# A fused audio tower (patches, attention, mixture of experts): one q/k projection per batch, its parts placed by SBUF transfers, and a new order of a cycle's work

## The chip, the cores and the metric

One core of a Trainium2 chip. The metric is the device time of one execution in microseconds; the kernel before takes 269.61 us (median of 3 runs, 268.11 to 270.89).

## What is computed

Sixteen batches of 512 frames with 128 features. Per batch: three strided patch embeddings (patches of 8, 16 and 32 frames, half overlapping) give N = 221 tokens of 128 features; pre-norm attention with 8 heads of 16 is added; then, for the first 1024 tokens of the flattened batch only (T = 1024, so batches 0 to 4), a dropless mixture of 8 experts with top 2 is added.

```python
h = concat([patches_i(x) @ W_i.T + b_i + pos_i + scale_emb[i] for i in range(3)], axis=1)   # (16, 221, 128)
q, k, v = split(layernorm(h) @ w_qkv.T)            # 8 heads of 16
attn = softmax(einsum('bhnd,bhmd->bhnm', q, k) / sqrt(16), axis=-1)
h = h + (attn @ v).reshape(...) @ w_agg.T + b_agg
xg = layernorm(h).reshape(-1, 128)[token_ids]       # T tokens, sorted by expert
y = where(bin_ids == e, gelu(xg @ w1[e]) @ w2[e], y)   # for each of 8 experts
h = h + scatter_add(w * y)
```

## The kernel before

Each engine has its own instruction stream, written by hand in program order; semaphores join them. After a prologue that loads x and the weights and computes the first three token units, all engines run the same loop over cycles c = -2 to 15. Cycle c holds the attention of batch c, split in two blocks of tokens (128 and 93, `TILE_N`), the embedding of later batches, and in c = 7 to 14 one round of experts, n = c - 7, of three tiles of 128 tokens (two in n = 7).

*Token matmuls.* `PLAN[c] = (p1, p2, pm, p3, p4)` says how many matmuls of the token units 3 to 8 (264 in all, `LEFT`) `tok_some` issues at five places of cycle c. Units 3, 5 and 8 have 508 columns, unit 4 252, unit 6 504, unit 7 248. A unit's last matmul lets VectorE copy it out (`hT_evac`), which a new unit waits for since all share `e_ps`; each unit goes through x_hi w_hi, x_hi w_lo, x_lo w_hi.

*Attention on TensorE.* `s1(c, blk)` forms the scores of one block to find the row maxima: four PSUM banks `s_ps`, all of them, so VectorE's `maxima(c, 0)` must end before `s1(c, 1)`, and `maxima(c, 1)` before `place_max(c)`, which turns the negated maxima into `m_ps[:, 2]`. VectorE's `take_max` adds them into the low part of q. `s2(c, blk)` forms the transposed scores with the maxima already subtracted, again in all four banks, so ScalarE's `exps(c, 0)` must end before `s2(c, 1)`, and `exps(c, 1)` before `s1(c+1, 0)`. `pv(c-1)`, `aggregate(c-1)` finish the batch before.

*High and low parts.* q and k are each split into a rounded part and the rest. Of 32 rows per head, `q_hi` holds q_hi twice, `k_a` k_hi and k_lo, `q_lo` q_lo and the maxima, `k_b` k_hi and a unit row. To get q and k twice, `project_q` and `project_k` multiply with doubled weights (two fp32 matmuls each; from batch 8 on q is projected once and doubled by `q_double`, two shuffles on VectorE). ScalarE makes `q_high`, `k_high`, VectorE `q_low`, `k_unit`, `k_low`.

*Layer norm of batch c+2.* `h_turn`, a copy, `ln_stats` (VectorE), `stage1` (GpSimd, rstd), `ln_z` (VectorE), `z_turn`, `zT_copy`. Up to batch 8 `ln_z(c+2)` stands in cycle c and `z_turn(c+1)` behind `s1(c, 0)`; later `ln_z(c+1)` and `z_turn(c+1)` stand in the middle of cycle c.

*Experts, round n.* `zs_turn(n)` transposes the gathered tokens, `zsT_evac(n)` copies them and derives `slot_w` and `idx_u`; `hidden(n, i)`, a gelu, `down`; ScalarE weighs y, GpSimd scatters it with indirect transfers and copies the experts' weights. SP loads the tokens: `load_zs(0)` in c = 6, `load_zs(1)` and `load_zs(2)` in c = 7, then `load_zs(n+2)`; from the second on each waits for `idx_ready` of the round before. SP's queue is in order: what stands behind a waiting instruction waits too.

Of the kernel before, what the change touches and what calls it, by code (L numbers as in the profile page):

```python
# [176 lines left out]
def build(nc, x0, x1, wt, pos, bias, wqkv, wagg, bagg, consts, ew, ei, w1, w2, z0, out):  # L177
    with ExitStack() as ctx:
# [28 lines left out]
        q_hi = sb("q_hi", [P, 2, 2, NE], F32R)  # L207
        q_lo = sb("q_lo", [P, 2, 2, NE], F32R)
        k_a = sb("k_a", [P, 2, 2, NE], F32R)
        k_b = sb("k_b", [P, 2, 2, NE], F32R)  # L210
# [1460 lines left out]
```

## Time and profile before

| | |
|---|---|
| time, median of 3 | 269.61 us |
| profiled execution, its own time | 267.78 us |
| its span, first to last instruction | 266.0 us |
| TensorE (PE) busy | 251.3 us, 94% |
| VectorE (DVE) busy | 217.1 us, 82% |
| ScalarE (ACT) busy | 149.4 us, 56% |
| GpSimd (POOL) busy | 127.9 us, 48% |
| mean granted TensorE clock | 0.996 |
| chain that ended last | PE 65%, DVE 24%, POOL 2%, ACT 2%, DMA 2% |

The span is that of the instructions; the execution's own time holds 1.8 us more around it. A busy share is an average over stages. Matmuls are pipelined, so their durations overlap: what one costs is read from start to start. TensorE's weight loads (PEld) run beside its matmuls. In the chain, time is given by the engine that each step was on, followed back from the last instruction.

### The profile page before, as it was taken

Reading aid. Unit: us, or ns where it says so; the run is one execution under the profiler, and the core shown is the slowest. Engines: PE = TensorE matmul, PEld = TensorE weight load, DVE = VectorE, ACT = ScalarE, POOL = GpSimd, SP = SyncE. Lnnn points to the kernel's source line nnn. Section 1 sums busy time; section 2 is a strip of 40 time slices with the busy share of each in tenths; the row PEclk is TensorE's granted clock in tenths of the full one; section 3 lists DMA queues with packets and bytes.
Section 4 is the critical chain, followed back from the end, with each engine's and each line's share of the span. In section 5 each row is a group of like instructions: output and inputs, shape, how many; then the busy total and the mean of one; then the engine's idle time right before and its main releaser. Section 6 shows DMA issues by size and latency. Waiting matters only on the chain.

```text
span 266.0 us, 7015 instructions
## 1 busy us (share of the span) xinstructions
PE 251.3 (94%) x2759; PEld 206.8 (78%) x2759; DVE 217.1 (82%) x474; ACT 149.4 (56%) x244; POOL 127.9 (48%) x178
## 2 busy tenths in 40 slices
PE   7999989999899999999999999999999999998991
PEld 7799867777576779887777988888888797876771
DVE  3994679879989989788886979798989898888742
ACT  4770332825261525343437978796969696878350
POOL 4000031103348474748575165667676766855422
PEclk9999999999999999999999999999999999999998
DMA  6999300089301010101111103031313122122122
GB/s 210 418 391 464 130 1 0 2 246 316 90 22 27 28 30 28 27 28 27 30 44 38 40 10 54 19 51 29 51 29 53 27 40 34 16 34 19 30 22 44
DMA packets 17151, 21.30 MB, mean 80 GB/s; under 512 B 2392, under 2 KB 12224, under 8 KB 17088
## 3 DMA queue, kind: packets, MB, share of 16 engines
q1 hardware_dynamic: 12400, 17.68, 20.0%
q0 software_dynamic: 4336, 2.60, 7.9%
q10 hardware_dynamic: 384, 0.57, 0.7%
q8 instruction: 22, 0.36, 0.6%
q14 instruction: 9, 0.07, 0.1%
HBM read 16.44 MB, written 5.95 MB: 84 GB/s over the span
## 4 chain that ended last, share of the span: by engine, by line
PE 65%; DVE 24%; POOL 2%; DMA 2%; ACT 2%; issue 2%; SPq 0%; DVEq 0%; POOLq 0%; ACTq 0%
PE e_ps L1194 12%; PE s_ps L1286 10%; PE s_ps L1194 8%; PE m_ps L1400 7%; PE m_ps L1467 5%; DVE nmax L959 4%; PE m_ps L1268 3%; DVE k_b L935 3%; PE m_ps L1258 2%; PE e_ps L1482 2%; PE e_ps L1467 2%; DMA x_raw<-x 2%; DVE x_lo L821 2%; DVE o_tok L985 1%; PE m_ps L1374 1%
## 5 line engine op out<-in xcount | busy, mean ns | idle before, releaser
L959 DVE TENSOR_REDUCE nmax<-s_ps 128x4 fp32r<-128x884 f32 (+1 forms) x60 | 61.7, 1069 | 8.5 <-PE s_ps L1286 8.3
L632 ACT ACTIVATE probs<-s_ps 128x888 f32<-128x888 f32 (+1 forms) x60 | 51.2, 904 | 20.2 <-PE s_ps L1286 20.2
L527 POOL DMA_INDIRECT out<-y_sb,idx_u x23 | 36.9, 1602 | 26.4 <-DMA out<-y_sb,idx_u 23.5
L465 POOL TENSOR_TENSOR var_eps<-mv,eps_t 128x2 f32<-128x2 f32 x16 | 8.5, 531 | 62.7 <-DVE mv L914 62.6
L498 POOL DMA_INDIRECT z_slots<-z,slot_u x20 | 23.4, 1172 | 15.3 <-PE s_ps L1286 11.0
L1400 PE MATMUL m_ps<-probs,v_aug 128*32 128x221 f32 (+1 forms) x480 | 25.8, 353 | 0.0
L1482 PE MATMUL e_ps<-w_now,hidT 128*128 128x128 f32 x184 | 23.2, 276 | 0.0
L1286 PE MATMUL s_ps<-k_a,q_hi 32*128 32x222 f32 (+1 forms) x252 | 19.1, 309 | 3.7 <-DVE q_lo L929 2.2
L1482 PEld LDWEIGHTS e_ps<-w_now,hidT 128*128 128x128 f32 x184 | 22.4, 192 | 0.1
L1286 PEld LDWEIGHTS s_ps<-k_a,q_hi 32*128 32x128 f32 (+1 forms) x252 | 11.9, 169 | 12.5 <-issue 5.7
L693 ACT ACT_TABLE_LOAD x16 | 20.5, 1283 | 0.3
L473 POOL TENSOR_TENSOR hb<-h_sb,bagg_sb 128x256 f32<-128x256 f32 x16 | 11.7, 734 | 18.4 <-DVE z_sb L919 18.4
L1400 PEld LDWEIGHTS m_ps<-probs,v_aug 128*32 128x32 f32 (+1 forms) x480 | 14.0, 109 | 7.1
L1194 PE MATMUL e_ps<-x_hi,w_hi 128*128 128x248 f32 (+3 forms) x88 | 19.5, 349 | 0.0
L614 ACT COPY zT<-m_ps 128x221 f32<-128x221 f32 x16 | 5.5, 345 | 24.3 <-PE m_ps L1245 24.3
L1194 PE MATMUL e_ps<-x_hi,w_lo 128*128 128x248 f32 (+3 forms) x88 | 19.1, 345 | 0.0
L538 POOL COPY w_now<-w_sb 128x512 f32 x23 | 17.5, 891 | 2.6 <-issue 1.3
L973 DVE SCALAR_TENSOR_TENSOR q_lo<-q_lo,c_sb,m_ps 128x442 fp32r<-128x442 f32 x15 | 10.1, 675 | 9.3 <-PE m_ps L1374 9.3
L1194 PE MATMUL e_ps<-x_lo,w_hi 128*128 128x248 f32 (+3 forms) x88 | 17.7, 339 | 0.0
L1467 PE MATMUL m_ps<-zsT,w_now 128*128 128x128 f32 x120 | 16.9, 284 | 0.3 <-DVE zsT L1061 0.3
L549 POOL COPY w_now<-w_sb 128x512 f32 x23 | 16.8, 1025 | 0.4
L1286 PE MATMUL s_ps<-k_b,q_lo 16*128 16x222 f32 (+1 forms) x252 | 16.4, 267 | 0.0
(181 smaller groups left out, 602.2 us busy)
## 6 DMA issues: line engine op xcount, KB each, us to landing
w_raw<-wt SPq DMA_DIRECT2D x6, 512.0 KB, 9.8
x_raw<-x SPq DMA_DIRECT2D x6, 512.0 KB, 10.9
w_sb<-w SPq DMA_DIRECT2D x1, 2048.0 KB, 9.7
z_slots<-z SPq DMA_DIRECT2D x1, 1518.0 KB, 15.0
zs<-z_slots SPq DMA_DIRECT2D x7, 198.0 KB, 2.5
x_raw<-x SPq DMA_DIRECT2D x4, 256.0 KB, 5.3
out<-h SPq DMA_DIRECT2D x11, 64.0 KB
c_sb<-consts SPq DMA_DIRECT2D x1, 600.0 KB, 13.1
```

The costliest lines, as they stand in the source:

```text
L498: g.indirect_dma_start(z_dram, bass.IndirectOffsetOnAxis(ap=slot_u[0:n, col:col + 1], axis=0), z2[0:n, b % 2, t, k, :], None).then_inc(sca ...
L527: g.indirect_dma_start(rows, bass.IndirectOffsetOnAxis(ap=idx_u[:, at:at + 1], axis=0), y_sb[:, n % 2, i, :], None, compute_op=ALU.add).th ...
L538: g.tensor_copy(w1_now[:, i, :], w1_sb[:, bass.ds(e, 1), :].rearrange("p a f -> p (a f)")).then_inc(w1_ready, 1)
L549: g.tensor_copy(w2_now[:, i].rearrange("p c d -> p (c d)"), w2_sb[:, bass.ds(e, 1), :, :].rearrange("p a c d -> p (a c d)")).then_inc(w2_r ...
L632: s.activation(probs[0:n, blk, 2 * f:2 * f + 2].rearrange("p t u n -> p t (u n)"), s_ps[0:n, 2 * f:2 * f + 2, 0:2 * NE], ACT.Exp, scale=DH ...
L693: s.activation(warm[func][:], c_sb[:, C_SGN:C_SGN + 1], func)
L959: v.tensor_reduce(nmax[0:n, blk, 2 * f:2 * f + 2, DH:DH + 2], src, AX_X, ALU.max, negate=True).then_inc(max_ready, 1)
L1194: mm = pe.matmul(dst, w_part[:, t, :], src, start=((u, k, i, c) == at_piece[0]), stop=((u, k, i, c) == at_piece[-1]))
L1286: mm = pe.matmul(dst[0:n, i, u * NE:(u + 1) * NE], a[rs, u, P * blk:P * blk + n], b[rs, u, :], start=start, stop=stop)
L1400: mm = pe.matmul(m_ps[32 * t:32 * t + 32, 0, r * N:(r + 1) * N], v_aug[0:n, b % 2, blk, HALF * r + t, :], probs[0:n, blk, t, r, 0:N], star ...
L1467: mm = pe.matmul((e_ps if i % 2 else m_ps[:, 1])[:, c * P:(c + 1) * P], w1_now[:, i, c * P:(c + 1) * P], zsT[:, i, :], start=True, stop=True)
L1482: mm = pe.matmul(e_ps[:, i * P:(i + 1) * P], hidT[:, i, c, :], w2_now[:, i, c, :], start=(c == 0), stop=(c == FC - 1))
```

## The change

q and k are projected once, side by side (`project_qk`, two fp32 matmuls into one bank), and split once into `qk` = (q_hi, k_hi, q_lo, k_lo): `qk_high` on ScalarE, `qk_low` on VectorE. Six transfers per batch, issued by SP (`place_qk`), put these parts into the rows of `pair_a` (even rows q_hi and k_hi, odd rows q_hi and k_lo) and `pair_b` (even rows k_hi and q_lo; the unit rows are set once by `set_units`). `k_high`, `k_unit`, `k_low`, `q_double` are gone. `take_max` now writes `q_max`, so `s1` and `s2` read different tensors. The low products use 32 rows instead of 16. Blocks are of 104 and 117 tokens. The experts' weights are loaded in four pieces in cycles 1 to 4. On TensorE `pv` stands directly between the two halves of `s1`, with the tokens behind; `hidden(n+1, 0)` and `z_turn(c+2)` end the cycle; `PLAN` is new. `ln_stats`, `ln_z`, `v_copy` and, for n >= 0, `keep_h` move, and aggregate's result lies in bank 0, so `pv(b)` waits for the residual of b - 1. A line of "..." stands for what is left out.

```diff
-N0, N1 = P, N - P
+N0 = 104
+N1 = N - N0
...
-PLAN = {-2: (3, 11, 0, 0, 0), -1: (2, 4, 0, 1, 3), 0: (18, 8, 0, 10, 12), 1: (2, 5, 2, 5, 10), 2: (2, 5, 2, 5, 10),
-        3: (2, 5, 2, 5, 10), 4: (4, 10, 4, 10, 20), 5: (4, 10, 4, 10, 20), 6: (2, 5, 2, 5, 10)}
+PLAN = {-2: (3, 11, 0, 0, 0), -1: (4, 6, 0, 16, 20), 0: (4, 8, 0, 6, 10), 1: (2, 6, 2, 5, 6), 2: (3, 7, 2, 4, 6),
+        3: (4, 9, 4, 8, 8), 4: (4, 10, 4, 8, 14), 5: (4, 8, 4, 8, 12), 6: (2, 5, 2, 5, 10)}
...
+            def place(b, pair, odd, u, parts):
+                half = HALF * DH
+                to, of = pair[odd:P:2, b % 2, u], qk[half * u:half * (u + 1), parts]
+                sp.dma_start(to.bitcast(F32), of.bitcast(F32)).then_inc(qk_placed[b % 2], 16)
+            def place_qk(b):
+                sp.wait_ge(qk_hi_ready, b + 1)
...
+                    sp.wait_ge(s2_done, 2 * b - 2)
+                for u in range(2):
+                    place(b, pair_a, 0, u, slice(0, 2))
+                sp.wait_ge(qk_lo_ready, b + 1)
+                for u in range(2):
+                    place(b, pair_a, 1, u, slice(0, 4, 3))
+                for u in range(2):
+                    place(b, pair_b, 0, u, slice(1, 3))
...
-            for c in range(BATCH + 1):
+            for c in range(-1, BATCH + 1):
                 n = c - E0
+                if c + 1 < BATCH:
+                    place_qk(c + 1)
+                if 1 <= c <= EXPERTS // 2:
+                    load_experts(2 * c - 2, 2 * c)
...
+            def qk_high(b):
+                act.wait_ge(qk_done, b + 1)
+                if b:
+                    act.wait_ge(qk_placed[(b - 1) % 2], 16 * PLACES * ((b - 1) // 2 + 1))
+                s.copy(qk[:, 0:2, 0:N], qk_ps()).then_inc(qk_hi_ready, 1)
...
+            def qk_low(b):
+                dve.wait_ge(qk_hi_ready, b + 1)
+                if b:
+                    dve.wait_ge(qk_placed[(b - 1) % 2], 16 * PLACES * ((b - 1) // 2 + 1))
+                v.tensor_tensor(qk[:, 2:4, 0:N], qk_ps(), qk[:, 0:2, 0:N].bitcast(F32),
+                                ALU.subtract).then_inc(qk_lo_ready, 1)
...
                 if c == BATCH - 1:
                     nmaxT_copy(c)
-                elif c >= 0:
-                    take_max(c)
+                elif c >= -1:
+                    qk_low(c + 1)
+                    if c >= 0:
+                        take_max(c)
...
                 if here:
                     s1(c, 0)
-                if ahead1 and c + 1 < LATE_Z:
-                    z_turn(c + 1)
-                if n > 0:
-                    hidden(n, 0)
                 if behind:
                     pv(c - 1)
-                tok_some(p1)
                 if here:
                     s1(c, 1)
-                if ahead1 and c + 1 >= LATE_Z:
-                    z_turn(c + 1)
+                tok_some(p1)
                 if n == 0:
                     zs_turn(0)
-                    project_q(c + 1)
+                else:
+                    hidden(n, 1)
+                if ahead1:
+                    project_qk(c + 1)
+                if n == 0:
                     hidden(n, 0)
-                hidden(n, 1)
+                    hidden(n, 1)
                 hidden(n, 2)
-                if ahead1 and n != 0:
-                    project_q(c + 1)
-                hidden(n, 3)
...
                 if here:
                     s2(c, 0)
-                if ahead1:
-                    project_k(c + 1)
                 tok_some(p3)
...
                 tok_some(p4)
+                if n >= 0:
+                    hidden(n + 1, 0)
+                if ahead2:
+                    z_turn(c + 2)
```

TensorE, cycle 4, from `pv(3)` to `aggregate(3)`, before. `L1194` are token matmuls, `L1258` and `L1268` the projections of q and k, `L1236` and `L1237` h_turn, `L1374` place_max; `s_ps<-k_a,q_hi` is s1, `s_ps<-q_hi,k_a` s2.

```order
L1400 MATMUL m_ps<-probs,v_aug 32x221 x16
L1194 MATMUL e_ps<-x_hi,w_hi 128x248 x4
L1286 MATMUL s_ps<-k_a,q_hi 93x222 x4
...
L1194 MATMUL e_ps<-x_hi,w_hi 128x248 x4
L1286 MATMUL s_ps<-q_hi,k_a 128x222 x8
L1286 MATMUL s_ps<-q_lo,k_b 128x222 x8
L1268 MATMUL m_ps<-zT,wqkv_sb 128x221 x2
L1194 MATMUL e_ps<-x_hi,w_hi 128x248 x10
L1286 MATMUL s_ps<-q_hi,k_a 93x222 x8
L1286 MATMUL s_ps<-q_lo,k_b 93x222 x8
L1430 MATMUL m_ps<-wagg_sb,o_T 128x128
```

The same place of the changed kernel; `L1381` is pv, `L1253` project_qk, `L1353` place_max, `L1410` aggregate.

```order
L1381 MATMUL m_ps<-probs,v_aug 32x221 x16
L1268 MATMUL s_ps<-pair_a 117x222 x4
...
L1194 MATMUL e_ps<-x_hi,w_hi 128x248 x4
L1253 MATMUL m_ps<-zT,wqkv_sb 128x221 x2
...
L1353 MATMUL m_ps<-ident_r,nmax 128x118
L1194 MATMUL e_ps<-x_hi,w_lo 128x248 x4
L1268 MATMUL s_ps<-pair_a 104x222 x8
L1268 MATMUL s_ps<-q_max,pair_b 104x222 x8
L1194 MATMUL e_ps<-x_hi,w_lo 128x248 x8
L1268 MATMUL s_ps<-pair_a 117x222 x8
L1268 MATMUL s_ps<-q_max,pair_b 117x222 x8
L1410 MATMUL m_ps<-wagg_sb,o_T 104x128
```

Nothing stands between pv and s1's second half now, and between s2's halves k's projection and two of ten token matmuls are gone.

SP's queue around cycle 7, before (`L410` and `L413` store h, `L420` is load_zs, the one in the middle load_zs(1) and load_zs(2)):

```order
L420 DMA zs<-z_slots 128x3x132 [waits scattered1,scattered0]
L410 DMA out<-h 128x128 [waits h1_ready]
L413 DMA out<-h 93x128
L420 DMA zs<-z_slots 128x3x132 [waits slot_w_ready,idx_ready,zs_turned] x2
L410 DMA out<-h 128x128 [waits h1_ready]
```

And of the changed kernel (`L414` is place):

```order
L450 DMA zs<-z_slots 128x3x132 [waits scattered1,scattered0]
L440 DMA out<-h 104x128 [waits h1_ready]
L443 DMA out<-h 117x128
L414 DMA pair_a<-qk 64x444 [waits s2_done,qk_hi_ready]
L414 DMA pair_a<-qk 64x444
L414 DMA pair_a<-qk 64x2x222 [waits qk_lo_ready]
L414 DMA pair_a<-qk 64x2x222
L414 DMA pair_b<-qk 64x444 x2
L450 DMA zs<-z_slots 128x3x132 [waits slot_w_ready,idx_ready,zs_turned] x2
L440 DMA out<-h 104x128 [waits h1_ready]
```

The six transfers of batch 8 now stand ahead of load_zs(1) and load_zs(2).

TensorE at the end of cycle 2 of the changed kernel, from aggregate(1) to the first scores of batch 3; `x_lo,w_hi` are the first token matmuls of unit 6 that read x_lo:

```order
L1410 MATMUL m_ps<-wagg_sb,o_T 104x128
L1411 MATMUL m_ps<-wagg_sb,o_T 117x128
L1259 MATMUL m_ps<-wqkv_sb,zT 104x128
L1260 MATMUL m_ps<-wqkv_sb,zT 117x128
L1194 MATMUL e_ps<-x_hi,w_lo 128x504 x3
L1194 MATMUL e_ps<-x_lo,w_hi 128x504 x3
L1242 MATMUL m_ps<-c_sb,z_sb 128x104
L1243 MATMUL m_ps<-c_sb,z_sb 128x117
L1268 MATMUL s_ps<-pair_a 104x222 x4
```

In the kernel before, the x_lo matmuls of unit 6 begin in cycle 3; here three of them stand ahead of batch 3's first scores, and z_turn(4) behind them.

## Rows read from the trace of the kernel before

**Rows 1.** Busy time by stretch of cycles: length, engines, clock, DMA share.

```profile
core 0: us, PE busy (x) PEld busy (x) DVE busy (x) ACT busy (x) POOL busy (x), PEclk, DMA share, GB/s
40.35:53.16 12.81, 12.12 (x131) 10.54 (x132) 12.12 (x28) 6.97 (x10) 1.86 (x4) 1.00 0.01 1
53.16:136.84 83.68, 82.77 (x902) 63.94 (x901) 72.49 (x157) 33.68 (x54) 44.31 (x64) 1.00 0.24 72
136.84:151.62 14.78, 14.23 (x171) 11.72 (x170) 12.25 (x29) 10.05 (x16) 4.90 (x8) 1.00 0.21 50
151.62:234.54 82.92, 80.32 (x1002) 68.68 (x1001) 72.91 (x160) 66.20 (x117) 57.39 (x71) 1.00 0.23 34
```

**Rows 2.** Timeline of cycle 4: start, duration, engine, operation.

```profile
95.52 0.38 PE L1286 MATMUL s_ps<-k_a,q_hi 32*128 32x222 f32 x4
...
96.29 2.06 DVE L959 TENSOR_REDUCE nmax<-s_ps 128x4 fp32r<-128x884 f32 x2
...
98.81 0.35 PE L1286 MATMUL s_ps<-k_a,q_hi 32*93 32x222 f32 x4
...
102.52 0.49 PE L1286 MATMUL s_ps<-q_hi,k_a 32*128 32x222 f32 x8
...
103.24 1.01 PE L1268 MATMUL m_ps<-zT,wqkv_sb 128*128 128x221 f32 x4
...
103.36 1.72 ACT L632 ACTIVATE probs<-s_ps 128x888 f32<-128x888 f32 x2 [2.11 <-PE s_ps L1286]
...
105.34 0.45 PE L1286 MATMUL s_ps<-q_hi,k_a 32*93 32x222 f32 x8
```

**Rows 3.** Chain that ended last, merged: start, duration, what.

```profile
58.25 1.13 PE e_ps L1194 x5
...
96.58 1.64 PE m_ps L1400 x32
...
99.47 0.94 PE m_ps L1258 x4
100.63 1.16 PE e_ps L1194 x10
```

**Rows 4.** Timeline, TensorE, cycle -1.

```profile
35.36 1.01 PE L1258 MATMUL m_ps<-zT,wqkv_sb 128*128 128x221 f32 x4
```

**Rows 5.** Timeline, cycle 2: the second half of s1, VectorE's tail.

```profile
71.03 0.35 PE L1286 MATMUL s_ps<-k_a,q_hi 32*93 32x222 f32 x4 [0.58 <-DVE nmax L959]
...
77.62 0.25 DVE L914 BATCH_NORM_AGGREGATE mv<-stats 128x2 f32<-128x6 f32 x2
...
79.41 0.60 DVE L919 TENSOR_SCALAR z_sb<-h_sb,mv,rstd 128x128 f32<-128x128 f32 x2 [0.30 <-POOL rstd L467]
...
80.26 1.65 DVE L821 TENSOR_TENSOR x_lo<-x_raw,x_hi 128x1024 fp32r<-128x1024 f32 x1
```

**Rows 6.** Timeline of cycle 7; then the answer on tile zs: issue, landing.

```profile
141.89 0.22 DVE L1063 TENSOR_SCALAR idx_u<-zs,c_sb 128x3 uint32<-128x3 f32 x1
...
142.18 0.38 SPq L420 DMA_DIRECT2D zs<-z_slots  x1
...
144.72 0.55 PE L1450 MATMUL e_ps<-c_sb,zs 128*128 128x128 f32 x3
...
L420 SPq DMA_DIRECT2D zs<-z_slots x8: 371/372/380, 137.0 to 215.1; - x8
...
DMA to landing us min/median/max: 2.1/2.5/3.7
```

**Rows 7.** Timeline, cycle 10 and the start of 11.

```profile
186.98 0.55 DVE L1061 COPY zsT<-e_ps 128x384 f32<-128x384 f32 x1
...
188.02 1.95 PE L1482 MATMUL e_ps<-w_now,hidT 128*128 128x128 f32 x16
...
192.93 0.19 PEld L1286 LDWEIGHTS s_ps<-k_a,q_hi 32*128 32x128 f32 x4 [0.59 <-DVE q_lo L929]
```

**Rows 8.** Timeline, VectorE, cycle 13.

```profile
223.55 0.61 DVE L919 TENSOR_SCALAR z_sb<-h_sb,mv,rstd 128x128 f32<-128x128 f32 x2 [0.98 <-POOL rstd L467]
```

More of the change, by code:

```diff
@@ L203, in build @@
         zT = sb("zT", [P, N])
[L207 to L210, printed above, removed]
+        qk = sb("qk", [P, 4, NE], F32R)
+        pair_a = sb("pair_a", [P, 2, 2, 2, NE], F32R)
+        pair_b = sb("pair_b", [P, 2, 2, 2, NE], F32R)
+        q_max = sb("q_max", [P, 2, NE], F32R)
         v_aug = sb("v_aug", [P, 2, 2, HEADS, 32])
@@ L297, in build, with q_hi, k_a, q_lo @@
             "p (b t u n) -> p b t u n", b=2, t=HALF, u=2)
-        def q_src(b):
-            return q_d[:] if b >= DOUBLED else m_ps[:, 0, 0:2 * N].rearrange("p (u n) -> p u n", u=2)
+        def q_hi(b):
+            return pair_a[:, b % 2, :, 0]
+        def k_a(b):
+            return pair_a[:, b % 2, :, 1]
+        def q_lo(b):
+            return pair_b[:, b % 2, :, 1]
+        def k_b(b):
+            return pair_b[:, b % 2, :, 0]
+        def qk_ps():
+            return m_ps[:, 0, 0:2 * N].rearrange("p (w n) -> p w n", w=2)
+        def agg_bank(b):
+            return e_ps[:, 2 * P:4 * P] if b == BATCH - 2 else m_ps[:, 0, 2 * P:4 * P]
         def pair_of(banks):
@@ L451, in _ @@
             g.memset(mhalf_t[:], -0.5)
-            for part in (q_hi, q_lo, k_a, k_b):
-                g.memset(part[:, :, :, N:NE].bitcast(F32), 0.0)
+            g.memset(qk[:, :, N:NE].bitcast(F32), 0.0)
+            g.memset(q_max[:, :, N:NE].bitcast(F32), 0.0)
+            g.memset(pair_b[:].bitcast(F32), 0.0)
             g.memset(nmax[:].bitcast(F32), 0.0)
@@ L594, in _ @@
                 scatter_y(n - 1, 2)
+                if n >= 0 and c + 2 < BATCH:
+                    keep_h(c + 2)
                 if 0 <= b < FFN_B - 1:
@@ L1302, in s1 @@
                 for u in range(2):
-                    four(s_ps, q_hi[:, b % 2], k_a[:, b % 2], blk, u, True, False)
-                    mm = four(s_ps, q_lo[:, b % 2], k_b[:, b % 2], blk, u, False, True, rows=DH)
+                    four(s_ps, q_hi(b), k_a(b), blk, u, True, False)
+                    mm = four(s_ps, q_lo(b), k_b(b), blk, u, False, True)
                 mm.then_inc(s1_done, 1)
@@ L1322, in s1_pair @@
                 for u in range(2):
-                    four(dst, q_hi[:, b % 2], k_a[:, b % 2], blk, u, True, False, heads)
-                    mm = four(dst, q_lo[:, b % 2], k_b[:, b % 2], blk, u, False, True, heads, DH)
+                    four(dst, q_hi(b), k_a(b), blk, u, True, False, heads)
+                    mm = four(dst, q_lo(b), k_b(b), blk, u, False, True, heads)
                 mm.then_inc(s1_done, 1)
```

250 lines of the change are left out of this document (89 added, 161 removed).

## The prediction

> **What bounds the kernel now.** I read the stretches first, then TensorE's timeline of one cycle of each kind, then the chain. A cycle runs from one s1(c,0), the first scores' first half, to the next. [rows 1] give the cycles: c0 12.81 us, c1 to c6 83.68, c7 14.78, c8 to c13 82.92; PE is busy for 82.77 of the 83.68 and 80.32 of the 82.92, at clock 1.00 throughout. So PE's instruction stream, in its written order, sets the pace; the others count only where PE has nothing to issue. One such place recurs late: s1(c,0) waits 0.59 for q_lo at the end of VectorE's k_b, k_a, q_lo tail [rows 7].
>
> **Prices.** On PE: pv 1.64; q or k projection 0.94 in the chain, 0.69 between starts (103.24 to the token matmuls after it), so I take 0.7; a token matmul 0.115 (248 or 252 columns) or 0.23 (504 or 508) [rows 3]. The two chained dependencies of a cycle are in [rows 2]: VectorE starts the maxima 0.77 after s1(4,0) starts and needs 2.06, so s1(c,1) cannot start before 0.77 + 2.06 + 0.06 = 2.89 after s1(c,0); and ScalarE's two exps start 0.84 after s2(4,0) and take 1.72, so s2(c,1), which reuses their banks, cannot start before 2.6 after s2(c,0). Before, PE covers both: z_turn, pv and tokens fill the first (s1(4,1) stands at 3.29), k's projection and 10 tokens the second (105.34 - 102.52 = 2.82).
>
> **What the change does to them.** It saves PE one projection of 0.7 per cycle up to c6 (four matmuls become two) and one matmul of about 0.37 later. VectorE loses k_b, k_a, the shuffles and gains one v copy; ScalarE loses k_a. That relief pays only where PE waited for it, the 0.59 of [rows 7]. Against it stand four costs.
>
> *1. Cycles -1 and 0: +4.0.* 46 instead of 10 token matmuls stand in c = -1. From the projection at 35.36 [rows 4]: 0.85 + 0.14 (h_turn) + 6 x 0.23 + 0.4 (v) + about 0.6 (hT_evac of unit 3, which now gates unit 4) + 36 x 0.115 + 0.33 (z_turn) puts s1(0,0) at 43.3 instead of 40.35 [rows 1]: +3.0. The six transfers hide here: q/k are split by about 37.6, the last issue is near 39, and landing within 4 is early enough. In c0 the 18 tokens between the halves are gone, so PE stands 2.25; lo_x behind the maxima delays the second maxima to 6.35. Adding the pieces: 0.64 + 2.25 + 0.59 + 0.5 + 0.99 + 1.0 + wait 0.4 + 0.26 + s2 with its wait 1.4 + 1.55 + 0.35 + 0.59 + 0.46 + 2.45 + 0.33 = 13.8 for 12.81: +1.0. Some of this is work moved, credited next.
>
> *2. c1 to c6: +2.6.* Off: six k projections, -4.2, and the moved tokens (29.2 of work for 32.8), -3.6. On: the first dependency is covered by s1 (0.64) and pv (1.64) alone, so PE waits 2.89 - 2.28 = 0.6 in each, +3.6. The second is covered by 4 to 8 tokens (0.9 to 1.3), leaving 0.6 to 0.85, +4.5. At c2 two VectorE effects come on top. The new order puts ln_stats, then the wait for GpSimd's rstd (77.87 to 79.41, 1.54, filled with k_b and k_a before, now empty), ln_z, v copy, lo_x (1.65) and the residual one behind the other [rows 5]; c1's tail then ends about 1.9 too late for the maxima of c2, and PE stands 0.6 + 1.9 ahead of s1(2,1), where it stood 0.58 before: beyond the 0.6 already counted, +1.3. And unit 6 started earlier, so its last three tokens of c2 are x_lo tokens: they wait for lo_x(9), which by the same addition ends 2.1 after PE gets there: +2.1. Sum -7.8 + 3.6 + 4.5 + 1.3 + 2.1 = +3.7. Adding starts along each cycle gives 2.2, since a block of tokens costs a gap at its borders, and some blocks are gone. I take 2.6, nearer the latter.
>
> *3. c7: +4.8.* The queue of SP is in order. load_zs(1) was issued at 142.18, 5.34 into the cycle, as soon as idx_u was there, and PE's zs_turn(1) ran at 144.72 just as it landed [rows 6]. Now it stands behind place_qk(8), whose third transfer waits for qk_low(8), which VectorE reaches behind the maxima of s1(7,1). These start behind zsT_evac(0) at about 5.2, end at 7.25, qk_low ends at 7.85; four issues at 0.37 put load_zs(1) at 9.35 and, landing in 2.5, at 11.85 (issue and landing: [rows 6]). PE is at zs_turn(1) at 8.4: it waits 3.4, and behind it on PE stand h_turn, s2(7,0), down and all the rest. After 11.85: 0.75 to s2(7,0) at 12.6, zsT 13.6, down 15.5, s2(7,1) 16.15, aggregate, v, down 18.5, then hidden(1,0) (0.96, moved in from c8) and z_turn 0.33: 19.6 for 14.78. load_zs(n+2) later is harmless: it is ready near 9.0, after the transfers are issued.
>
> *4. c8 to c13: +1.3.* Per cycle: -0.4 matmul, -0.5 of the wait for q_lo; +0.6 before s1(c,1); +0.15 for h_turn behind the third gelu; +0.4 before down, because zsT ends (186.98 + 0.55) and down used to start at 188.02 behind k's projection, which covered it [rows 7]. Together +0.3, +1.7 over six; c13's own 1.0 wait for rstd [rows 8] may go, hence 1.3.
>
> *5. c14: -1.0.* hidden(7,0) has moved to c13 and the waits ahead of s1(15,0) go. The tail is left as it is (0).
>
> Edits at nothing: N0 = 104 (a half costs PE 0.64 or 0.59, so the mean stays), 32 rows instead of 16 in the low products, the new order of zT, o_raw and the gelus on ScalarE (busy 66.20 of 82.92 in c8 to c13 [rows 1]), set_units in the prologue, where VectorE waits for the counts; if that cover fails it costs about 1. Weight loads in four pieces: they follow each cycle's transfers by half a cycle.
>
> **The transfers.** The trace has no SBUF-to-SBUF transfer. Nearest rows: zs, 198 KB, lands in 2.1 to 3.7 [rows 6], against 114 KB each here. From the last issue (about 8 into a cycle) to the next s1 there are 5 us: at 2.1 or 3.7 they cost nothing. Free below 5, each us above costs 15. The Trainium skill, "DMA: Bandwidth & Descriptors", Rules for kernel authors, warns that two transfers to disjoint partition halves serialize on the same engines; its fit in the section on the anatomy of one DMA (2.0 us plus bytes over 436 GB/s) makes, as an estimate of that page, 2.3 for one and about 3.6 for all six in series. By the page or by the zs row the sum is the same, but the rule is what would feed the second rival.
>
> **Sum.** 4.0 + 2.6 + 4.8 + 1.3 - 1.0 = +11.7: a span of 277.7 for 266.0. The profiled execution took 267.78, 1.83 below the median 269.61 of the runs shown; with the same difference the median becomes 281.3, said 281.
>
> **Rivals.** *PE work and VectorE relief decide (faster).* 22 fp32 projection matmuls at 0.37 are 8 us, five late waits of 0.6 another 3: 269.6 - 11 = 259. It needs PE not to stand ahead of s1(c,1) and s2(c,1); it decides if the two reductions take under 1.5 together instead of 2.06 and the exps under 1.0 instead of 1.72. The rows speak against it. A milder form, half the waits of parts 2 and 4 filled and no wait in c7: 281 - 4.8 - 7 = 269, no change. *The transfers land late (slower still).* At 7 us instead of under 4, 15 cycles wait 2: 281 + 30 = 311; at 5.5, 288. For it: six at once, 682 KB; against: 5 us of room. *GpSimd's rstd is late.* z_turn is now needed in the cycle of its ln_stats; as in c13 [rows 8], 1.0 for seven cycles: 288. Against: keep_h is now behind the last scatter, so stage1 can start by about 10. *load_zs(1) is not late*, everything else as forecast: 276.
>
> **Chances.** Forecast with its own range 276 to 286: 0.58. Without the c7 wait, 271 to 277: 0.12. Late rstd or transfers: 0.10. No change: 0.09. Faster: 0.11. A measurement of this kernel tells about 1% from no change. Faster by over 1% (under 267) 0.12, within 1% (to 272.3) 0.11, slower 0.77. Range 268 to 288.
>
> **What would show it.** s1(0,0) near 43; PE idle about 0.6 ahead of each s1(c,1), released by nmax, and 0.6 to 0.85 ahead of s2(c,1) in c1 to c6, released by probs; in c2 a wait of token matmuls for x_lo; in c7 one wait of over 3 us of zs_turn for the zs transfer, issued behind six transfers; cycles 8 to 13 near 14.1. Wrong if s1(c,0) waits for transfers, if z_turn waits for z_sb every cycle, or if the second halves start without a gap.

## The result, and the profile after

Four executions of the changed kernel took 283.24 us (282.32 to 285.85), four of the kernel before on the same chip 268.86 (268.01 to 270.89): ratio 1.054, 95% interval 1.044 to 1.064. It is slower, by 14.4 us where 11.7 were forecast. The profiled execution took 283.87 with a span of 281.8, against 266.0 before. Some executions of a kernel, whatever the kernel, run at a lower granted clock than its others, and the ratios leave them out: one of five of a3_fill and one of two of a4_late_places (the profiled one of each), two of ten of b2_plan_tok_zs, two of four of b3_and_hidden, two of six of c1_all_filled, and one of the eleven of the kernel before that ran beside it.

The first lines of the page after: span, busy time of the engines, and the clock of TensorE in 40 slices of 7 us.

```profile
span 281.8 us, 6982 instructions
...
PE 244.3 (87%) x2711; PEld 202.4 (72%) x2711; DVE 191.2 (68%) x420; ACT 140.2 (50%) x220; POOL 124.8 (44%) x177
...
PEclk9999999898899999999999689999999999999998
```

The stretches that answer to [rows 1]: cycle 0, cycles 1 to 6, cycle 7, cycles 8 to 13 (columns: bounds, length, busy time and instructions of PE, PEld, DVE, ACT, POOL, granted clock, DMA share, GB/s).

```profile
44.43:58.99 14.56, 11.82 (x107) 9.57 (x106) 10.58 (x24) 6.47 (x9) 1.71 (x3) 0.88 0.21 48
58.99:144.93 85.94, 73.84 (x862) 57.79 (x861) 63.19 (x144) 30.68 (x48) 39.14 (x63) 0.98 0.44 117
144.93:167.70 22.77, 17.02 (x178) 14.62 (x177) 11.36 (x26) 10.49 (x17) 7.95 (x14) 0.85 0.28 65
167.70:252.11 84.41, 76.87 (x990) 65.51 (x989) 61.07 (x133) 61.66 (x102) 57.34 (x69) 1.00 0.44 83
```

The change does take work off TensorE: 73.84 us in cycles 1 to 6 where [rows 1] had 82.77 (3.6 of the 8.9, by the prediction's price, are the 16 token matmuls dealt to earlier cycles). But 12.1 us of these cycles are now idle where 0.9 were. Who is waited for stands in the waits of the page after, TensorE's own, largest first (line of the instruction that waits, the one that releases it: us in total, times, longest):

```profile
PE s_ps L1268 <- DVE nmax L968: 10.0, 14, 2.2
PE e_ps L1430 <- DMA zs<-z_slots: 5.2, 1, 5.2
PE e_ps L1194 <- DVE hT L825: 4.4, 3, 1.8
PE s_ps L1268 <- ACT probs L663: 4.2, 7, 0.7
PE e_ps L1462 <- DVE zsT L1070: 2.7, 6, 0.5
PE m_ps L1236 <- ACT hidT L715: 1.6, 6, 0.4
PE e_ps L1194 <- DVE x_lo L840: 1.3, 1, 1.3
```

The same place as [rows 2] after, cycle 4 on TensorE, shows the two dependencies with their empty stretches, 0.63 for the maxima and 0.70 for the exps:

```profile
105.70 0.35 PE L1268 MATMUL s_ps<-pair_a 32*104 32x222 f32 x4
...
108.62 0.37 PE L1268 MATMUL s_ps<-pair_a 32*117 32x222 f32 x4 [0.63 <-DVE nmax L968]
...
112.70 0.46 PE L1268 MATMUL s_ps<-pair_a 32*104 32x222 f32 x8
...
113.36 1.18 PE L1194 MATMUL e_ps<-x_hi,w_lo 128*128 128x248 f32 x8
115.24 0.47 PE L1268 MATMUL s_ps<-pair_a 32*117 32x222 f32 x8 [0.70 <-ACT probs L663]
```

And cycle 7, which alone costs 8.0 us more than before: the chain of waits through it (start, length, what).

```profile
145.65 2.07 DVE nmax L968 x2
...
150.91 1.06 DVE nmax L968
151.97 0.54 DVE qk L953
152.52 0.62 SPq L414
153.13 0.04 issue
153.18 0.61 SPq L414
...
153.83 0.60 SPq L414
...
154.47 0.60 SPq L414
...
155.18 2.74 DMA zs<-z_slots
157.92 0.04 issue
157.96 0.90 PE e_ps L1430 x3
...
160.36 3.75 PE e_ps L1462 x16
```

Maxima, qk_low, four transfers of q and k, the transfer of zs, and only then zs_turn(1): as forecast. Not forecast is the last row: 16 matmuls of down take 3.75 us where [rows 7] have 1.95 for the same 16. The granted clock in the stretch behind the wait is 0.50 (1.2 GHz) for 6 us:

```profile
158.00:160.00 2.00, 2.00 (x21) 1.76 (x21) 0.67 (x2) 0.00 (x0) 0.00 (x0) 0.50 0.00 0
160.00:162.00 2.00, 1.93 (x16) 1.68 (x13) 1.90 (x10) 1.66 (x2) 0.75 (x2) 0.50 0.19 33
162.00:164.00 2.00, 2.00 (x10) 1.82 (x9) 1.22 (x4) 0.06 (x1) 1.45 (x3) 0.50 0.28 77
164.00:166.00 2.00, 2.00 (x29) 1.84 (x29) 0.18 (x1) 1.21 (x2) 0.06 (x1) 0.98 0.00 0
```

The account of the profiled executions, in us:

| stretch | before | after | difference | forecast |
|---|---|---|---|---|
| up to s1(0,0) | 40.35 | 44.43 | +4.1 | +3.0 |
| cycle 0 | 12.81 | 14.56 | +1.75 | +1.0 |
| cycles 1 to 6 | 83.68 | 85.94 | +2.3 | +2.6 |
| cycle 7 | 14.78 | 22.77 | +8.0 | +4.8 |
| cycles 8 to 13 | 82.92 | 84.41 | +1.5 | +1.3 |
| cycle 14 | 12.04 | 11.66 | -0.4 | -1.0 |
| tail | 19.42 | 18.03 | -1.4 | 0 |
| span | 266.0 | 281.8 | +15.8 | +11.7 |

### The profile page after: what moved, and what is told of

It reads as the page before. It is cut to its first block, busy times and chain, and to the rows that moved or that the text cites. A ratio compares the mean times of both kernels' runs of the same rounds, so it can differ in the third digit from the quotient of the medians.

```text
span 281.8 us, 6982 instructions
## 1 busy us (share of the span) xinstructions
PE 244.3 (87%) x2711; PEld 202.4 (72%) x2711; DVE 191.2 (68%) x420; ACT 140.2 (50%) x220; POOL 124.8 (44%) x177
## 4 chain that ended last, share of the span: by engine, by line
PE 66%; DVE 18%; ACT 5%; issue 4%; DMA 3%; SPq 1%; POOL 1%; DVEq 0%; POOLq 0%; ACTq 0%
PE s_ps L1268 13%; PE e_ps L1194 13%; DVE nmax L968 10%; PE e_ps L1462 8%; PE s_ps L1194 8%; PE m_ps L1253 4%; PE m_ps L1447 4%; ACT probs L663 3%; PE e_ps L1447 3%; DMA x_raw<-x 2%; PE m_ps L1410 2%; ACT hidT L715 1%; PE m_ps L1259 1%; PE m_ps L1381 1%; PE m_ps L1260 1%
## 5 line engine op out<-in xcount | busy, mean ns | idle before, releaser
L968 DVE TENSOR_REDUCE nmax<-s_ps 104x4 fp32r<-104x884 f32 (+1 forms) x60 | 61.9, 1073 | 29.2 <-PE s_ps L1268 29.1
L663 ACT ACTIVATE probs<-s_ps 104x888 f32<-104x888 f32 (+1 forms) x60 | 51.3, 907 | 40.3 <-PE s_ps L1268 39.8
L1268 PE MATMUL s_ps<-pair_a 32*104 32x222 f32 (+1 forms) x504 | 34.9, 311 | 15.1 <-DVE nmax L968 10.0
L1268 PEld LDWEIGHTS s_ps<-pair_a 32*104 32x104 f32 (+1 forms) x504 | 21.3, 172 | 30.7 <-DVE nmax L968 15.7
L1381 PE MATMUL m_ps<-probs,v_aug 104*32 104x221 f32 (+1 forms) x480 | 25.8, 353 | 0.0
L1194 PE MATMUL e_ps<-x_hi,w_hi 128*128 128x248 f32 (+3 forms) x88 | 20.1, 361 | 4.4 <-DVE hT L825 4.4
L1194 PE MATMUL e_ps<-x_lo,w_hi 128*128 128x248 f32 (+3 forms) x88 | 19.0, 353 | 1.3 <-DVE x_lo L840 1.3
L657 ACT CAST qk<-m_ps 128x442 fp32r<-128x442 f32 x16 | 8.5, 529 | 22.6 <-PE m_ps L1253 22.3
L1381 PEld LDWEIGHTS m_ps<-probs,v_aug 104*32 104x32 f32 (+1 forms) x480 | 14.0, 109 | 7.1
L938 DVE TENSOR_SCALAR z_sb<-h_sb,mv,rstd 128x128 f32<-128x128 f32 x32 | 11.1, 389 | 11.2 <-POOL rstd L502 11.2
L1194 PEld LDWEIGHTS e_ps<-x_hi,w_hi 128*128 128x128 f32 x88 | 13.4, 197 | 6.9 <-DVE hT L825 5.1
L1194 PE MATMUL e_ps<-x_hi,w_lo 128*128 128x248 f32 (+3 forms) x88 | 18.3, 340 | 0.0
L1268 PE MATMUL s_ps<-pair_b 32*117 32x222 f32 (+1 forms) x264 | 17.2, 260 | 0.0
```

Of the source, the lines that this page charges most:

```text
L663: s.activation(probs[0:n, blk, 2 * f:2 * f + 2].rearrange("p t u n -> p t (u n)"), s_ps[0:n, 2 * f:2 * f + 2, 0:2 * NE], ACT.Exp, scale=DH ...
L968: v.tensor_reduce(nmax[0:n, blk, 2 * f:2 * f + 2, MAX_ROW[0]:MAX_ROW[1] + 1:2], src, AX_X, ALU.max, negate=True).then_inc(max_ready, 1)
L1194: mm = pe.matmul(dst, w_part[:, t, :], src, start=((u, k, i, c) == at_piece[0]), stop=((u, k, i, c) == at_piece[-1]))
L1268: mm = pe.matmul(dst[0:n, i, u * NE:(u + 1) * NE], a[rs, u, N0 * blk:N0 * blk + n], b[rs, u, :], start=start, stop=stop)
L1381: mm = pe.matmul(m_ps[32 * t:32 * t + 32, 0, r * N:(r + 1) * N], v_aug[0:n, b % 2, blk, HALF * r + t, :], probs[0:n, blk, t, r, 0:N], star ...
```

## The experiments

All but one start from the changed kernel. They ran in three groups, each beside the kernel before: 268.33 us with the a kernels, 267.74 with the b kernels, 266.86 with the c kernels (268.86 beside the changed kernel itself). A difference between kernels of two groups is therefore good to 1 or 2 us, and small ones are read from the traces. The theory throughout is that four things that the new order exposes make the loss, each by itself: the queue of SP in cycle 7, the maxima, the new table of tokens, and the clock behind a long wait.

**a1_zs_first: the queue of SP alone.**

```diff
+                if n == 0:
+                    load_zs(1)
                 if c + 1 < BATCH:
                     place_qk(c + 1)
...
-                if n == 0:
-                    load_zs(1)
```

> Only SP's order is changed: load_zs(1) is issued ahead of the six transfers of place_qk(8). Theory (the 5.2 us wait of zs_turn(1) in cycle 7, and the fall of TensorE's granted clock from 1.00 to 0.50 behind it, both come from load_zs(1) standing behind qk_low(8) in the queue): the wait is under 0.5 us, the granted clock stays at 1.00 in cycle 7, cycle 7 falls from 22.8 us to 15 to 16, and the whole to 276 us. Rival 1 (the wait goes but the clock falls anyway): cycle 7 at 17.5 to 18, 278.5 us. Rival 2 (cycle 7 is bound by VectorE's chain of maxima, qk_low and take_max, and the transfers of q and k now land late): a new wait of 2 us or more takes the place, 281 us or above.

277.35 us (275.71 to 278.85), 5.9 less than the changed kernel; the wait of zs_turn(1) is gone and the clock holds in cycle 7. A wait of 0.59 is left there, of zs_turn(0) for its own load. Cycle 7 is 16.22 long:

```profile
145.75:161.97 16.22, 14.37 (x177) 12.12 (x176) 11.08 (x26) 10.36 (x17) 7.93 (x14) 1.00 0.38 91
```

So 6.55 of the 8.0 us of cycle 7 were this order. Elsewhere the profiled executions differ in where the clock fell: here in cycle 3, behind the 1.83 us wait for hT (17.91 us long for 15.58, clock 0.82), but not in cycle 0 (13.41 for 14.56). Together that is 1.2 us against this run, which is why its span gained 5.6, less than cycle 7 alone.

**a3_fill: is it the idle stretch that lowers the clock?**

```diff
+                if n == 0:
+                    for _ in range(FILL):
+                        pe.matmul(s_ps[:, 0, 0:P], zero[:], zero[:], start=True, stop=True)
                 if n >= 0:
                     zs_turn(n + 1)
```

> 21 matmuls of a 128x128 tile of zeros into a free bank are put ahead of zs_turn(1) in cycle 7, where TensorE stands still for 5.15 us (they do nothing else). Theory (the granted clock falls to 0.50 behind that stretch because TensorE was idle in it, and the matmuls of the next 6 us, from zs_turn(1) to down, take twice their time): the zeros fill 4.7 us of the wait at 0.22 us each, zs_turn(1) ends when it did, the granted clock stays at 1.00, and cycle 7 is 3 us shorter: 280.2 us. Rival (the clock falls for another cause than the idle time): no gain, 283 us, or slower by what the zeros overrun.

The zeros fill 4.91 us, 1.26 stay empty, and the clock is 1.00 in the whole cycle. The first row is the zeros and the rest of the wait, the second goes from zs_turn(1) to the next s1:

```profile
152.16:158.33 6.17, 4.91 (x44) 4.72 (x44) 0.61 (x1) 2.08 (x3) 0.00 (x0) 1.00 0.47 110
158.33:165.77 7.44, 6.96 (x80) 6.29 (x80) 4.54 (x16) 4.31 (x7) 3.04 (x6) 1.00 0.15 36
```

From zs_turn(1) to s1(8,0) it takes 7.44 where the changed kernel took 9.74 (157.96 to 167.70): the clock behind the wait costs 2.3 us. The cycle is only 1.45 shorter (21.32 for 22.77), since the zs transfer landed 0.85 later in it. The whole, 282.63, is not distinguishable from 283.24, and falls of the clock elsewhere differ from execution to execution. So the mechanism is shown in the stretch, the forecast gain in the whole is not. (The profiled execution took 291.78: from 263 us on its clock stands near 0.5 for some 20 us. What is read from it lies ahead of that.) The Trainium skill, "TensorE: Matmul & The Clock Gate", section on what is actually happening, says that activity is what releases the clock and idleness what throttles it; this pair agrees.

**a2_tokens_between: cover for the maxima.** In cycles 0 to 6 the first block of tokens stands ahead of s1(c,1).

```diff
                     pv(c - 1)
+                tok_some(p1)
                 if here:
                     s1(c, 1)
-                tok_some(p1)
```

> Only TensorE's order is changed: in cycles 0 to 6 the first token block (2 to 4 matmuls) stands ahead of s1(c,1), between pv and it, and not behind it. Theory (s1(c,1) waits 0.53 to 0.93 us for the first maxima because pv alone is too short to cover them): the wait ahead of s1(c,1) falls by the block's length, 0.23 to 0.9 us, to under 0.2 in cycles 1 to 6, and from 2.2 to about 1.6 in cycle 0; in all -3.5 us, 279.8 us. Rival (the chain on VectorE, maxima, qk_low, take_max, bounds the cycle anyway, so what is won ahead of s1(c,1) is waited for ahead of s2(c,0) or s2(c,1)): within 1 us of the changed kernel, 283 us.

280.54 us (279.63 to 282.27), 2.7 less. Not one wait for the maxima of over 0.2 is left in cycles 1 to 6; in cycle 0 it is 1.51 instead of 2.17. But the rival has a share. Cycle 1 is 1.36 shorter, most of it because the clock held where it had fallen; cycles 2 to 6 are shorter by 0.67, 0.39, 0.35, 0.06 and 0.25, less than the tokens moved into the waits. In cycle 5 these rows are s1(5,1) and place_max(5):

```profile
118.11 0.37 PE L1268 MATMUL s_ps<-pair_a 32*117 32x222 f32 x4
...
120.96 0.43 PE L1353 MATMUL m_ps<-ident_r,nmax 104*128 104x104 f32 x2
```

They stand 2.85 apart where the changed kernel had 3.06, and 2.84 or 2.85 in cycles 4 and 6 too (3.30 and 3.28): that is the time which the second maxima need, so place_max now waits for them, in steps too short to stand among the waits. The theory holds for where the time was lost; the forecast was 0.8 too high because part of the cover only moved the wait.

**a4_late_places: how much room the transfers had.**

```diff
                 sp.wait_ge(qk_hi_ready, b + 1)
+                if b and b - 1 != E0:
+                    sp.wait_ge(s2_done, 2 * b)
```

> The six transfers of q and k for batch c+1 are held back until both halves of s2(c) are done, some 4 to 5 us later than before (not in cycle 7, whose zs transfer stands behind them). It measures how much room they have. Theory (the last of the six lands about 1.5 us behind its issue, as the DMA's busy share ends in cycle 5, so that in the changed kernel they have 1.5 to 3 us of room and cost nothing): s1(c,0) now waits 2.3 us in cycles 8 to 14 and 3.0 us in cycles 1 to 6 for the transfers, +37 us, 320 us. Rival (they land 3.7 us behind the last issue, as the slowest zs transfer of the kernel before, and are already at the edge in the changed kernel): 4.5 to 5.2 us each, 350 us.

Two executions, 344.39 and 350.92: in the whole the 350 of the rival and not the 320 of the theory, so the waits of TensorE have to decide between them:

```profile
PE s_ps L1270 <- DMA pair_b<-qk: 44.7, 14, 4.1
```

That is 3.2 each, a little above the theory (2.3 to 3.0) and far from the rival's 4.5 to 5.2. The rest of the loss, some 20 us, goes with a mean clock of 0.872 in the profiled execution; the theory had no term for it. On SP's queue the last issues for batch 1 and s1(1,0) on TensorE:

```profile
58.45 1.26 SPq L414 DMA_DIRECT2D pair_b<-qk  x2
```

```profile
61.47 0.36 PE L1270 MATMUL s_ps<-pair_a 32*104 32x222 f32 x4 [2.44 <-DMA pair_b<-qk]
```

The last of the six lands 1.76 us behind the end of its issue here, 1.75 to 2.5 in the other cycles. In the changed kernel the issues end at 127.95 in cycle 5 and at 191.44 in cycle 9, and s1 follows at 131.14 and 195.88. With the landings of the same cycles here, 1.8 and 2.1, that is room for 1.4 and 2.3 us. They are hidden, but by much less than I had thought, and at one place not at all: ahead of s1(15,0) the last issue ends at 262.00.

```profile
263.77 0.35 PE L1268 MATMUL s_ps<-pair_a 32*104 32x222 f32 x2 [0.29 <-issue]
```

The 1.77 between them is a landing time; in a1_zs_first, a3_fill and b2_plan_tok_zs the profile names the transfers as what s1(15,0) waits for, for 0.80 to 0.92. The Trainium skill, "DMA: Bandwidth & Descriptors", section on the anatomy of one DMA, has a fit for a transfer issued by GpSimd that gives 2.3 for one of this size (an estimate of mine from it); these are issued by SP, and the 1.75 to 2.5 lie around it. Six of them in series by its rule would be about 3.6 (the same estimate); here 3.7 us of issues (below) plus 1.75 make about 5.5 from first issue to last landing, so issuing is the larger part of what they take.

**b1_plan: the table of tokens alone.**

```diff
-PLAN = {-2: (3, 11, 0, 0, 0), -1: (4, 6, 0, 16, 20), 0: (4, 8, 0, 6, 10), 1: (2, 6, 2, 5, 6), 2: (3, 7, 2, 4, 6),
-        3: (4, 9, 4, 8, 8), 4: (4, 10, 4, 8, 14), 5: (4, 8, 4, 8, 12), 6: (2, 5, 2, 5, 10)}
+PLAN = {-2: (3, 11, 0, 0, 0), -1: (2, 4, 0, 1, 3), 0: (18, 8, 0, 10, 12), 1: (2, 5, 2, 5, 10), 2: (2, 5, 2, 5, 10),
+        3: (2, 5, 2, 5, 10), 4: (4, 10, 4, 10, 20), 5: (4, 10, 4, 10, 20), 6: (2, 5, 2, 5, 10)}
```

> The changed kernel with only PLAN as in the kernel before: 10 instead of 46 token matmuls in cycle -1, 48 instead of 28 in cycle 0, and every unit again ends at a cycle's end, not in its middle. Theory (the changed table costs time by itself: the next unit's tokens wait for hT_evac, which stands on VectorE behind both maxima, 0.78 + 1.84 + 1.83 us, x_lo is late for 1.3, and s2(c,1) waits up to 0.7 for the exps): all these waits go, s1(0,0) stands near 43 us since it now waits for the six transfers, whose issues end at 41.4, the wait of 2.2 us ahead of s1(0,1) stays; cycle 7 starts near 140.3 instead of 144.9: 278.6 us. Rival (the tokens are only work moved, and the waits sit where the tokens were taken from): within 1.5 us of the changed kernel, 283 us.

279.58 us (279.31 to 280.85), 3.7 less, or 2.5 less when each kernel is taken against the kernel before that ran beside it. s1(0,0) stands at 42.99 and waits for the transfers, as expected; the waits for hT and x_lo are gone:

```profile
42.99 0.52 PE L1268 MATMUL s_ps<-pair_a 32*104 32x222 f32 x4 [2.28 <-DMA pair_b<-qk]
...
46.23 0.54 PE L1268 MATMUL s_ps<-pair_a 32*117 32x222 f32 x4 [2.18 <-DVE nmax L968]
```

Cycles 1 to 6 take 13.57 to 13.93 each, 81.99 together, where the changed kernel took 85.94 with 16 token matmuls fewer. Cycle 0 is 17.10 long, with a mean clock of 0.72 behind the two waits. Cycle 7, where nothing was changed, is 21.43 for 22.77, because the clock behind its wait of 5.1 fell for a shorter time; so 1.3 us of this execution's gain are not the table's. What this table takes away in one place is the mid-cycle end of a unit. In the changed kernel units 5 and 6 end in the middle of cycles 1 and 3; cycle 3 on VectorE and on TensorE:

```profile
97.97 0.61 DVE L983 TENSOR_TENSOR q_max<-pair_b,m_ps 128x442 fp32r<-128x442 f32 x1 [1.26 <-PE m_ps L1353]
98.51 0.64 DVE L993 STREAM_TRANSPOSE o_tok<-o_raw 128x448 f32<-128x448 f32 x1
99.07 0.65 DVE L825 TENSOR_TENSOR hT<-e_ps,comb 128x504 f32<-128x504 f32 x1
```

```profile
97.61 0.33 PE L1353 MATMUL m_ps<-ident_r,nmax 104*128 104x104 f32 x2
99.77 0.74 PE L1194 MATMUL e_ps<-x_hi,w_hi 128*128 128x248 f32 x4 [1.83 <-DVE hT L825]
```

The tokens of the next unit use the same bank, and its evacuation stands behind take_max and turn on VectorE: 1.83 us of nothing. In the kernel before every unit ended at a cycle's end and no such wait exists.

**b5_before_plan: the same table in the kernel before.** The same four lines the other way round, in the kernel before.

> The kernel before with only PLAN of the changed kernel. Theory (the table alone costs time: unit ends in mid-cycle, 46 tokens in cycle -1, too few in cycle 0): s1(0,0) +3 us, a wait for hT of 1.8 in cycles 1 and 3, x_lo late by 1 in cycle 2, s1(0,1) waits 1.5; the tokens moved ahead are saved later; cycle 7 starts 7 to 8 us later than in the kernel before: 276 us. Rival (the table hurts only with a single projection and pv alone ahead of s1(c,1)): within 2 us of the kernel before, 270 us.

277.48 us (276.68 to 278.51), ratio 1.032 (1.025 to 1.040) to the kernel before: 9.7 us slower through the table alone. The waits for hT (3.8 in two) and x_lo (2.2) stand there too, s1(0,1) waits 1.33. Cycle 7 starts 11.0 later than in the kernel before, not 7 to 8, with a mean clock of 0.90 in cycles 1 and 3. So the table costs with either kernel. Taking it back in the changed kernel gained only 3.7, because there the 46 tokens of cycle -1 had also covered the six transfers, which b1_plan waits for.

**c2_n128: the blocks.** `N0 = 104` back to 128, alone.

> The changed kernel with only the blocks of tokens as in the kernel before, 128 and 93 instead of 104 and 117. Theory (the split costs and brings nothing: columns per matmul, 221 or 222, stay, and a half costs 0.64 or 0.59 us either way): within 1 us of the changed kernel, 283 us. Rival (the even split shortens a chain on VectorE or ScalarE, or fewer rows are cheaper): 285 us or more here.

283.82 us (282.85 to 286.88). The ratio to the kernel before, 1.063 (1.055 to 1.071), overlaps the changed kernel's 1.054, but the times alone would not exclude the rival's 2 us. The traces do: cycles 1 to 6 take 85.87 for 85.94, cycle 7 22.74 for 22.77, cycles 8 to 12 14.12 or 14.13 each for 14.09. The blocks make no difference, as forecast.

**b2_plan_tok_zs: do the waits add up?** The edits of b1_plan, a2_tokens_between and a1_zs_first together.

> Three edits to the changed kernel: PLAN as before, the first token block ahead of s1(c,1) in cycles 0 to 6, and load_zs(1) ahead of place_qk(8). Theory (the four waits are separate and add up): no wait of over 0.6 us between cycles 0 and 6 but the one of s1(0,0) for transfers, s1(0,1) covered by 18 tokens, the clock at 1.00 all the way, cycle 7 starts near 135 and cycle 8 near 151 instead of 167.7: 266.4 us, a little under the kernel before. Rival (with the waits gone the six transfers, last landing about 1.5 us behind the last issue, get late, or VectorE's chain binds): 270 us or above.

Ratio 1.007 (1.003 to 1.011), near 270 us (eight executions, 268.50 to 271.01). About 12 of the 14.4 us are back. Cycle by cycle it came out as the theory has it (cycles 1 to 6 at 13.3 to 13.6, cycle 7 at 15.56), but not in cycle 0, which ran at clock 0.78 behind waits of 1.00 and 2.10 for z and the transfers:

```profile
42.66:57.34 14.68, 13.92 (x127) 12.19 (x127) 10.35 (x24) 6.12 (x8) 1.70 (x3) 0.78 0.21 48
```

The forecast of 266.4 had no such term. Where transfers that had been covered by 46 tokens are uncovered, they are waited for: here the rival has its point. It has another in cycles 1 to 6, where place_max stands 2.84 to 2.97 behind s1(c,1), the length of the second maxima, as in a2_tokens_between. Cycles 10 and 11 took 0.2 and 0.7 more than the 14.09 of the others, behind late maxima; why was not tried.

**b3_and_hidden: cover in the late cycles.** To b2_plan_tok_zs:

```diff
                 tok_some(p1)
+                if n > 0:
+                    hidden(n, 1)
                 if here:
                     s1(c, 1)
                 if n == 0:
                     zs_turn(0)
-                else:
-                    hidden(n, 1)
```

> b2_plan_tok_zs, and in cycles 8 to 14 hidden(n,1) also stands ahead of s1(c,1), between pv and it. Theory (0.53 us of each of these cycles is the wait of s1(c,1) for the first maxima, which 0.98 us of hidden covers): cycles 8 to 13 fall from 14.09 to 13.6, 3 to 3.5 us less than b2_plan_tok_zs: 263 us. Rival (s1(c,1) starts 0.4 later, so qk_low, which stands behind its maxima, the transfers and the tail of the cycle move too, and nothing is won): 266.4 us as b2_plan_tok_zs.

Two executions, 266.07 and 269.20, are too few for a verdict on the whole. In the trace cycles 8 to 13 take 13.85 instead of 14.09: the wait of 0.53 is gone, but 0.34 of it is back ahead of place_max, which now waits for the later maxima. Half way between theory and rival.

**c1_all_filled: work in every empty place.** To b3_and_hidden, a new PLAN, zs_turn(0) ahead of s1(7,1), and zs_turn(n+1) ahead of place_max:

```diff
+PLAN = {-2: (3, 11, 0, 0, 0), -1: (4, 6, 0, 6, 10), 0: (16, 4, 0, 8, 4), 1: (2, 5, 2, 7, 8), 2: (3, 4, 2, 7, 8),
+        3: (2, 5, 2, 7, 8), 4: (4, 10, 4, 14, 16), 5: (4, 10, 4, 14, 16), 6: (2, 5, 2, 7, 8)}
...
-                if n > 0:
+                if n == 0:
+                    zs_turn(0)
+                elif n > 0:
                     hidden(n, 1)
                 if here:
                     s1(c, 1)
-                if n == 0:
-                    zs_turn(0)
...
-                if here:
-                    place_max(c)
                 if n >= 0:
                     zs_turn(n + 1)
+                if here:
+                    place_max(c)
```

> b3_and_hidden, with every wait that is left filled by work moved there: PLAN -1: (4, 6, 0, 6, 10), 0: (16, 4, 0, 8, 4) (16 tokens of unit 4 stand in the 3.3 us in which TensorE waited for z and for the transfers ahead of s1(0,0)), two to four tokens more between s2's halves in cycles 1 to 6, zs_turn(0) ahead of s1(7,1), zs_turn(n+1) ahead of place_max. Theory (each wait costs its length, and the 2 us ones also a stretch at half clock): s1(0,0) stays near 43 but with 16 tokens done, cycle 0 at 12 without a fall of the clock, cycles 1 to 6 at 12.9 for 13.35, cycle 7 at 15.0, cycles 8 to 13 at 13.6: 260 us where b3_and_hidden has 266. Rival (the cycles of 13.3 and 13.85 are bound by VectorE's chain or by the transfers, which then make s1(c,0) wait): 265 us or above, with waits for transfers or for q_max instead.

264.57 us, the median of six; the ratio to the kernel before, from four of 263.31 to 264.99, is 0.988 (0.982 to 0.994). The changed kernel, with its order repaired, is 1.2% faster than the kernel before: little, but clear of 1. Cycle 0, cycles 1 to 6, cycle 7, cycles 8 to 13:

```profile
42.83:55.66 12.83, 10.82 (x110) 9.12 (x111) 10.58 (x24) 6.26 (x9) 1.70 (x3) 0.87 0.24 54
55.66:133.78 78.12, 77.25 (x876) 59.18 (x877) 63.65 (x144) 30.42 (x48) 39.70 (x63) 1.00 0.49 129
133.78:149.62 15.84, 14.30 (x177) 12.29 (x176) 11.20 (x26) 10.36 (x17) 8.00 (x15) 1.00 0.40 93
149.62:232.56 82.94, 80.28 (x990) 66.94 (x990) 60.06 (x133) 61.60 (x102) 56.23 (x69) 1.00 0.42 84
```

Cycles 1 to 6 are 5.6 us shorter than in [rows 1], of which TensorE's saved work is nearly all; it is busy 77.25 of 78.12. It missed its 260. Cycle 0 ran at a mean clock of 0.87 behind a wait of 1.01 for the transfers and one of 1.13 for the maxima. In cycle 7 zs_turn(0), now ahead of s1(7,1), waits 0.79 for zs, and the cycle took 15.84 instead of 15.0. Cycles 8 to 13 stay at 13.8 for 13.6: they wait 0.43 for zsT, and place_max stands 2.85 behind s1(c,1), where the second maxima let it go.

## Why the prediction was right, and where it was off

The forecast was 281, slower, and 283.2 came, inside the range and its own inner range of 276 to 286. The signs of all terms but the tail were right; two were mis-sized, and some of the sum is two errors that cancel.

*Part 1, cycles -1 and 0.* Forecast +4.0, measured +5.8. My sum started at the projection's place in [rows 4], but p1 of cycle -1 had grown from 2 to 4 tokens too, which shifts the projection itself to 36.13 (+0.8), the evacuation hT was waited for by 0.78 ahead of unit 4 where 0.6 was put, and a token costs 0.122 in a block (16 in 1.94 to 1.97), not 0.115. In cycle 0 the wait of 2.17 stood where 2.25 was forecast; the clock that fell behind it, to 0.64 over 47.27 to 51.97, was not. In a1_zs_first, where it did not fall, cycle 0 took 13.41: less than the 13.8 forecast.

*Part 2, cycles 1 to 6.* +2.3 for +2.6, but the size is luck. Right were the waits ahead of s1(c,1), 0.53 to 0.93 for 0.6, and ahead of s2(c,1), 0.48 to 0.70 in cycles 2 to 6 for 0.6 to 0.85 (a2_tokens_between and c1_all_filled fill them). Wrong was cycle 2: s1(2,1) waits 0.93 where 2.5 was forecast, and the tokens wait 1.28 for x_lo where 2.1 was. I had charged VectorE's whole tail to cycle 2 as if cycle 1 had not been longer. And missing altogether were the two waits of 1.83 for hT in cycles 1 and 3, with a fall of the clock in cycle 1. The step that failed is the one that read PLAN as a count of matmuls only: which half a unit ends in decides where its evacuation stands on VectorE. For unit 3 in cycle -1 I had seen it ("which now gates unit 4"); units 5 and 6 I did not follow.

*Part 3, cycle 7.* +8.0 for +4.8, the mechanism exactly as forecast and confirmed by a1_zs_first. Two sizes were off. The issue of a q/k transfer costs SP 0.60 to 0.62, not the 0.37 of [rows 6], and the landing took 2.74 for 2.5, so zs_turn(1) started 13.0 into the cycle instead of 11.85; the wait was 5.2 for 3.4, since place_max had ended earlier than I put PE there. The other 2.3 us are the clock (a3_fill).

*Parts 4 and 5.* Cycles 8 to 13 +1.5 for +1.3: 14.09 each, 0.53 for the maxima, 0.25 behind the gelu, 0.47 for zsT. Cycle 14 -0.4 for -1.0, because s1(14,1) waits 0.76, s2 for q_max 0.63, and the waits ahead of s1(15,0), which were to go, left one of 0.29 in their place, with the transfers just landed. The tail, left at 0, is 1.4 shorter. The stretch behind VectorE's last step (279.02 to 281.8, before 261.55 to 266.0), where only the last stores stand, is 1.7 shorter; why was not tried.

*The transfers.* Hidden in cycles 0 to 13, as forecast, but "5 us of room" was wrong: with issues of 0.62 the last one ends 3.0 to 4.4 ahead of s1 in cycles 4 to 6 and 8 to 13, and after landing 1.3 to 2.4 us are left. Ahead of s1(15,0) nothing is left, and in b1_plan they bind ahead of s1(0,0). The 2.3 and 3.6 of the prediction come from a fit for transfers that GpSimd issues, and held no term for the issuing on SP, which is 3.7 for six.

*The rivals.* "No change" and "faster" needed waits to be filled that nothing filled; c1_all_filled, where the maxima and the exps are covered, comes out on the faster rival's side of the kernel before, at 264.57, though far from its 259. So its relief was real in part, and its condition the missing part. "GpSimd's rstd is late" did not happen: z_turn waits in no cycle from 0 on.

## What to carry to other kernels

Taking matmuls off the busiest engine pays only if enough other work still stands between each pair of dependent steps. Before it is done, list each pair (scores and maxima, second scores and exps) with the work that covers it, and hand the freed time to those places; then look at the next pair, since cover taken from behind one step may be what covered the other. A queue that issues in order is a schedule of its own: put a load that someone needs early ahead of one that waits for late data, whichever batch they belong to. And when work is re-dealt among slots, follow the ends of its units too, since each end gates the next unit through another engine's queue.
